# Causal attention pairs: one-pass maximum, joint weight sums, a triangle cap on VectorE and row sums of two key tiles on TensorE

## The chip, the cores and the metric

One Trainium2 chip, one of its cores. The metric is the time of one execution of the whole program in microseconds (us) on the device; the median of several runs counts.

## The reference

The program computes eight residual layers over `x` of 4 x 1024 x 128. The change touches the fifth, the latent causal attention, with 16 heads for each of 4 sequences of 1024 tokens:

```python
q = (x @ Wq + bq).reshape(Bv, Tv, N_HEAD, HEAD_DIM)
k = (x @ Wk + bk).reshape(Bv, Tv, N_HEAD, LATENT)
v = (x @ Wv + bv).reshape(Bv, Tv, N_HEAD, LATENT)
qc = jnp.einsum('bthd,dl->bthl', q, Wc)
att = jnp.einsum('bthl,bshl->bhts', qc, k) * SCALE
att = jnp.where(causal[None, None], att, -jnp.inf)
att = jax.nn.softmax(att, axis=-1)
y = jnp.einsum('bhts,bshl->bthl', att, v).reshape(Bv, Tv, N_HEAD * LATENT)
return y @ Wo + bo
```

The folded query and key have 8 numbers a head, the value 64. Softmax needs, for each of the 1024 queries, the largest score among the keys up to the query itself, the exponentials of the scores less this maximum, their sum, and their product with the values.

## The kernel before

The heads are worked off in 32 pairs. The function is `attend_pairs`; it writes out the program of each engine by hand (`tensor`, `vector`, `scalar`, `gpsimd`, `sync`), and each runs 35 steps n = 0 to 34. In step n the engines work on three pairs at once: pair n (first scores and maxima), pair n-2 (second scores, exponentials, products with the values, sums) and pair n-3 (its last products and its row sums). The instructions wait for each other through counting semaphores; each engine takes its own strictly in order.

For a pair, each of the two heads (h = 0, 1):

- **First scores**, L1594, called f0 to f15 here (8 query tiles of 128 for each head, in the order 3, 5, 1, 7, 2, 6, 0, 4): TensorE makes the scores of one query tile against all keys up to its end, 128 to 1024 columns of bf16. f(m) waits for maximum m-2, since two places in PSUM take turns.
- **Maximum**, VectorE: L1775 adds the triangle mask to the 128 columns on the diagonal in PSUM; after a wait L1777 reduces the whole row to its negated maximum. The mask add reads PSUM and one operand in SBUF.
- GpSimd splits the maxima into bf16 parts (L1797, L1799), TensorE turns them (L1638), and a DMA lays them into the query stack, so that the second scores come out with the maximum subtracted.
- **Second scores**, L1604, called s0 to s23: transposed, key tile by query half. There are 12 units u for a head pair, (key tile, query half) = (0,0), (0,1), (1,0), (1,1), (2,0), (2,1), (3,0), (3,1), (4,1), (5,1), (6,1), (7,1), with 512, 512, 384, 512, 256, 512, 128, 512, 512, 384, 256, 128 columns; s(2u+h) belongs to unit u. Units 0, 2, 4, 6, 8, 9, 10, 11 cross the diagonal; for each of their two matmuls L1608 adds a mask of 128 columns by a second matmul.
- **Exponential**, L1734, ScalarE: PSUM to fp32 weights in SBUF; units 0 and 1 go straight into the accumulator `acc`, the others into a ring `prob` of 5 units.
- **Products with the values**, L1620, called w0 to w5 (units 2c and 2c+1, both heads, fp32): w(c) waits until both units' exponentials are there.
- **Sums of weights**, L1526: GpSimd adds units 2 to 11 into `acc`, one head at a time, 20 instructions a pair. In the last pair VectorE does the second head, after everything else. A ring place is free when its unit has been added and multiplied.
- **Row sums**, L1630: TensorE multiplies `acc` by ones into four strips of 32 rows. ScalarE copies them out (L1751), as it does the products (L1717).

TensorE's order in a full step: f0, s0 to s2, f1, s3, w5 (pair n-3), s4, f2, s5, s6, f3, s7, f4, w0, f5, s8, s9, f6, row sums (pair n-3), s10, s11, f7, w1, s12, f8, s13, s14, f9, the turned shift, w2, f10, s15, f11, s16, s17, f12, s18, w3, s19, s20, f13, s21, f14, w4, f15, s22, s23.

`early.invert` (L2087, L2057, L2059) forms the reciprocals of the sums of the first three sequences on VectorE. `project_qkv` stands in front of the pairs in the same block and makes queries, keys and values; `wide_attention_output` follows.

Of the kernel before, what the change touches and what calls it, by code (L numbers as in the profile page):

```python
# [101 lines left out]
def make_constants(nc, S, pool, made):  # L102
# [21 lines left out]
    for m, sign in ((S.mask_qk, -1), (S.mask_kq, 1)):  # L124
        c.run(nc.gpsimd.memset(m[:], 0.0))
        c.run(nc.gpsimd.affine_select(out=m[:], in_=m[:], compare_op=ALU.is_ge, fill=MASKED, base=0,
                                      pattern=[[sign, P]], channel_multiplier=-sign))
# [410 lines left out]

def by_tile(v):

    return v.rearrange("p (t e) -> p t e", e=E)
# [354 lines left out]
def project_qkv(nc, S, space, wq, bq, scale, wk, bk, wv, bv, vd, ahead, v_room=None):  # L896
# [8 lines left out]
    xn = sb("xn", [P, 2, GROUP])  # L905
# [541 lines left out]
def attend_pairs(nc, S, space, early):  # L1447
# [11 lines left out]
    ADDS = 2 * (NU - FIRST)  # L1459
# [23 lines left out]
    (s1_mm, maxed, split, m_mm, m_read, s2_mm, exped, pv_mm, added, last_added, also_added, sum_mm, sum_read, o_read0, o_read1) = [  # L1483
        steps(n) for n in ("s1_mm maxed split m_mm m_read s2_mm exped pv_mm added last_added also_added sum_mm sum_read o_read0 "
# [5 lines left out]
    cleared, chain, qk_masked = sem("cleared"), sem("chain"), sem("qk_masked")  # L1490
# [11 lines left out]

    def bank(what, c):

        return S2 + (len(turns) * c + turns.index(what)) % RING2
# [5 lines left out]
    def wait_for_added(eng, j, n, h):  # L1511

        if j.c < NP - 1:
            added.wait(eng, j.times(ADDS, 2 * n + h))
# [3 lines left out]
    def add(eng, op_of, j, u, h):  # L1518
        kt, c = units[u]
        exped.wait(eng, j.times(2 * NU, 2 * u + h))  # L1520
        if kt == 1:
            pv_mm.wait(eng, j.times(2 * NU, 2 * c + h))
        else:
            wait_for_added(eng, j, units.index((kt - 1, c)) - FIRST, h)
        sums = acc[:, j.slot(2), h, c, offset(u):GROUP]
        op_of.tensor_tensor(sums, sums, weights(j, u, h), ALU.add).then_inc(added_for(j, h).sem, 1)  # L1526
# [37 lines left out]
    def attach(project):  # L1564
# [17 lines left out]
        def tensor(pe):  # L1582
# [15 lines left out]
            def second_scores(j, t):  # L1598
# [3 lines left out]
                diagonal = kt * P >= c * GROUP  # L1602
                wait_for_bank(pe, t, j.c)
                op = nc.tensor.matmul(ps[:, bank(t, j.c), o:GROUP], ks[j.slot(4)][:, h, kt * P:(kt + 1) * P],  # L1604
                                      qs[j.slot(4)][:, h, c * GROUP + o:(c + 1) * GROUP], start=True,
                                      stop=not diagonal)
                if diagonal:
                    op = nc.tensor.matmul(ps[:, bank(t, j.c), o:o + P], S.ident_b[:], S.mask_kq[:],  # L1608
# [1790 lines left out]
```

## Time and profile before

| | us |
|---|---|
| median of 3 runs | 3065.84 |
| lowest, highest run | 3062.51, 3071.13 |
| span of the profiled execution | 3008.7 |
| this layer's pairs in it | 1294 to 1962 |

What lies between the span (first to last instruction) and the run's time is outside the instructions. The profile's engines are PE (TensorE matmul), PEld (TensorE weight load), DVE (VectorE), ACT (ScalarE), POOL (GpSimd) and SPq (the queue that issues DMAs). Matmuls are pipelined, so their recorded times overlap; how long one holds TensorE is read from start to start. An operation's line is the line in the code above.

### The profile page before, as it was taken

Reading aid. Unit: us, or ns where it says so; the run is one execution under the profiler, and the core shown is the slowest. Engines: PE = TensorE matmul, PEld = TensorE weight load, DVE = VectorE, ACT = ScalarE, POOL = GpSimd, SP = SyncE. Lnnn points to the kernel's source line nnn. Section 1 sums busy time; section 2 is a strip of 40 time slices with the busy share of each in tenths; the row PEclk is TensorE's granted clock in tenths of the full one; section 3 lists DMA queues with packets and bytes.
Section 4 is the critical chain, followed back from the end, with each engine's and each line's share of the span. In section 5 each row is a group of like instructions: output and inputs, shape, how many; then the busy total and the mean of one; then the engine's idle time right before and its main releaser. Section 6 shows DMA issues by size and latency. Waiting matters only on the chain. (4 is left out here: it accounts for less than half of the span.)

```text
span 3008.7 us, 44190 instructions
## 1 busy us (share of the span) xinstructions
PE 2506.9 (83%) x13254; PEld 1086.0 (36%) x13254; DVE 2417.9 (80%) x4200; ACT 1891.9 (63%) x3760; POOL 1257.2 (42%) x1704
## 2 busy tenths in 40 slices
PE   6897799999999899969999999996846566666666
PEld 4544122222222354424444444375821111111366
DVE  7777888888888467878888888776459999999963
ACT  2213688888888521226666666604649999999864
POOL 2015433433334101529999999911732121200036
PEclk9999899999999899979999999996979999999879
DMA  4002322222233200642222222254221111111123
GB/s 101 1 1 88 93 75 74 74 74 74 75 106 108 58 1 1 209 158 81 82 87 87 88 89 89 81 210 137 78 80 42 44 41 43 42 43 32 36 73 90
DMA packets 193930, 229.15 MB, mean 76 GB/s; under 512 B 55824, under 2 KB 122128, under 8 KB 193248
## 3 DMA queue, kind: packets, MB, share of 16 engines
q1 hardware_dynamic: 158960, 193.15, 20.0%
q0 software_dynamic: 31360, 30.05, 3.9%
q10 hardware_dynamic: 3376, 3.15, 0.4%
q8 instruction: 109, 1.79, 0.2%
q14 instruction: 125, 1.02, 0.1%
HBM read 139.72 MB, written 87.95 MB: 76 GB/s over the span
## 5 line engine op out<-in xcount | busy, mean ns | idle before, releaser
L1349 DVE TENSOR_REDUCE neg_max<-ps 128x1 f32<-128x1024 f32 x512 | 602.0, 1219 | 98.7 <-PE ps L1242 90.4
L1322 ACT ACTIVATE prob<-ps 128x512 f32<-128x512 f32 x1024 | 556.3, 601 | 94.3 <-PE ps L1256 85.6
L2650 DVE TENSOR_REDUCE neg_max<-ps 128x1 f32<-128x1024 f32 x512 | 581.0, 1211 | 13.8 <-PE ps L2444 13.7
L1526 POOL TENSOR_TENSOR acc<-acc,prob 128x384 f32<-128x384 f32 (+1 forms) x630 | 572.3, 952 | 34.3 <-PE ps L1620 33.2
L2520 ACT ACTIVATE ps<-ps,neg_max 128x1024 f32<-128x1024 f32 x512 | 557.4, 1091 | 23.9 <-DVE neg_max L2650 23.0
L2444 PE MATMUL ps<-k_stack,q_stack 128*128 128x512 bf16 x1024 | 332.9, 413 | 236.7 <-ACT ps L2520 216.0
L1734 ACT ACTIVATE prob<-ps 128x512 f32<-128x512 f32 (+3 forms) x640 | 270.6, 474 | 216.0 <-PE ps L1608 159.1
L1777 DVE TENSOR_REDUCE neg_max<-ps 128x1 f32<-128x512 f32 (+7 forms) x512 | 388.0, 758 | 17.5
L1256 PE MATMUL ps<-q_stack,k_stack 128*128 128x512 bf16 x1024 | 312.2, 386 | 7.1 <-DMA k_low<-k_parts 4.9
L1266 PE MATMUL ps<-prob,v 128*32 128x512 f32 x2048 | 281.3, 621 | 0.9 <-ACT prob L1322 0.7
L2444 PEld LDWEIGHTS ps<-k_stack,q_stack 128*128 128x128 bf16 x1024 | 62.6, 99 | 501.8 <-ACT ps L2520 423.2
L1594 PE MATMUL ps<-k_stack,q_stack 72*128 72x512 bf16 (+3 forms) x768 | 216.3, 339 | 27.5 <-DVE neg_max L1777 17.4
L1775 DVE TENSOR_TENSOR ps<-ps,mask_qk 128x128 f32<-128x128 f32 x512 | 150.8, 294 | 98.5 <-PE ps L1594 95.1
L668 PE MATMUL ps<-f_wd,hT 128*128 128x512 f32 x512 | 227.3, 595 | 2.3 <-DVE other L807 2.3
L1620 PE MATMUL ps<-prob,v 128*64 128x512 f32 (+3 forms) x1280 | 228.0, 477 | 0.9 <-ACT prob L1734 0.9
L1604 PE MATMUL ps<-q_stack,k_stack 128*128 128x512 bf16 (+3 forms) x768 | 220.0, 330 | 0.9 <-ACT prob L1734 0.3
L1256 PEld LDWEIGHTS ps<-q_stack,k_stack 128*128 128x128 bf16 x1024 | 78.6, 97 | 322.1 <-ACT prob L1322 211.4
L1364 POOL TENSOR_TENSOR shift<-neg_max,zeros 128x8 bf16<-128x8 f32 x64 | 12.5, 195 | 417.8 <-DVE neg_max L1349 417.8
L1241 PE MATMUL ps<-k_stack,q_stack 64*128 64x512 bf16 x512 | 163.3, 391 | 18.9 <-DVE neg_max L1349 11.6
L1242 PE MATMUL ps<-k_low,q_low 64*128 64x512 bf16 x512 | 163.3, 391 | 0.0
L851 POOL TENSOR_TENSOR x_res<-x_res,other 128x128 f32<-128x128 f32 x64 | 29.7, 464 | 261.6 <-DVE other L807 261.6
L668 PEld LDWEIGHTS ps<-f_wd,hT 128*128 128x128 f32 x512 | 94.9, 190 | 115.3 <-issue 108.1
(365 smaller groups left out, 3932.7 us busy)
## 6 DMA issues: line engine op xcount, KB each, us to landing
q_stack<-q_parts SPq DMA_DIRECT2D x576, 48.0 KB
k_stack<-k_parts SPq DMA_DIRECT2D x576, 48.0 KB
o_quads<-o_out SPq DMA_DIRECT2D x64, 256.0 KB
v<-v_wide SPq DMA_DIRECT2D x32, 512.0 KB
o_pairs<-o_out SPq DMA_DIRECT2D x64, 256.0 KB
num<-o_pairs SPq DMA_DIRECT2D x8, 2048.0 KB, 8.5
q_parts<-parts SPq DMA_DIRECT2D x24, 384.0 KB, 2.5
k_parts<-parts SPq DMA_DIRECT2D x24, 384.0 KB, 2.7
```

The source lines that it names most:

```text
L668: op = nc.tensor.matmul(ps[:, YB + 2 * (k % 2) + half, :], hT[:, g % 2, f, k * P:(k + 1) * P], S.f0_wd[:, f, half * GROUP:(half + 1) * GROUP],
L1256: nc.tensor.matmul(ps[:, bank(n), :], ks[j.slot(4)][:, kt * P:(kt + 1) * P], qs[j.slot(4)][:, c * GROUP:(c + 1) * GROUP], start=True, stop ...
L1266: nc.tensor.matmul(ps[quad:quad + VW, OB, :], vs[j.slot(4)][:, :, kt], prob[:, n % RING, :], start=kt < 2, stop=kt >= KTS - 2).then_inc(pv ...
L1322: nc.scalar.activation(prob[:, m % RING, :], ps[:, bank(m), :], ACT.Exp).then_inc(exped.sem, 1)
L1349: nc.vector.tensor_reduce(neg_max[:, i.slot(2), m:m + 1], ps[:, first:first + 2, :].rearrange("p b n -> p (b n)"), AX.X, ALU.max, negate=T ...
L1526: op_of.tensor_tensor(sums, sums, weights(j, u, h), ALU.add).then_inc(added_for(j, h).sem, 1)
L1620: nc.tensor.matmul(ps[h * VD:(h + 1) * VD, OB + c, offset(u):GROUP], v, weights(j, u, h), start=kt == 0, stop=kt == (c + 1) * GROUP // P - ...
L1734: nc.scalar.activation(weights(j, u, h), ps[:, bank(t, j.c), offset(u):GROUP], ACT.Exp).then_inc(exped.sem, 1)
L1777: nc.vector.tensor_reduce(neg_max[:, i.slot(2), m // KTS, qt:qt + 1], ps[:, bank:bank + c + 1, :].rearrange("p b n -> p (b n)") [:, 0:(qt ...
L2444: op = nc.tensor.matmul(ps[:, bank, :], qs[n % 4][:, qt * P:(qt + 1) * P], ks[n % 4][:, c * GROUP:(c + 1) * GROUP], start=True, stop=True)
L2520: nc.scalar.activation(s, s, ACT.Exp, bias=neg_max[:, n % 2, qt:qt + 1], accum_out=sums[:, cols(n * KTS + qt, 1)]).then_inc(summed.sem, 1)
L2650: nc.vector.tensor_reduce(neg_max[:, n % 2, qt:qt + 1], ps[:, first:first + 2, :], AX.XY, ALU.max, negate=True).then_inc(maxed.sem, 1)
```

## The change

- The mask add and the reduction of a query tile become one VectorE instruction over the whole row: it adds a strip (zeros, and the triangle in its last 128 columns), negates, writes the row back to PSUM and leaves the minimum of it, which is the negated maximum.
- The mask matmuls L1608 go. Instead VectorE takes the minimum of the exponentials and a triangle (`cap_kq`: huge where the key is allowed, 0 elsewhere) in the 128 diagonal columns of both heads, in place, in SBUF. This is a "cap"; there are 8 in a pair, placed between the maxima by `caps_after` (cap 11 in front of maximum 1 of the next step). Products and sums of these units wait for the cap instead of the exponential.
- GpSimd adds units 2 to 9 alone, both heads in one instruction: 8 instead of 20 a pair. In the last pair it adds the first head, and VectorE the second, spread over the step.
- TensorE makes the row sums of units 10 and 11 from the weights themselves, by four more matmuls onto the row sums.
- ScalarE's exponentials of units 5 and 6 wait for the previous pair's row sums where they waited for its adds of units 10 and 11.
- `early.invert` moves to step 32, after maximum 10's place.
- The projection's `xn` takes the memory of `o_out`.

```diff
@@ make_constants
-    for m, sign in ((S.mask_qk, -1), (S.mask_kq, 1)):
-        c.run(nc.gpsimd.memset(m[:], 0.0))
-        c.run(nc.gpsimd.affine_select(out=m[:], in_=m[:], compare_op=ALU.is_ge, fill=MASKED, base=0,
+    c.run(nc.gpsimd.memset(S.mask_strip[:], 0.0))
+    c.run(nc.gpsimd.memset(S.cap_kq[:], -MASKED))
+    for m, sign, fill in ((S.mask_strip[:, SEQ - P:SEQ], -1, MASKED), (S.cap_kq[:], 1, 0.0)):
+        c.run(nc.gpsimd.affine_select(out=m, in_=m, compare_op=ALU.is_ge, fill=fill, base=0,
                                       pattern=[[sign, P]], channel_multiplier=-sign))
+def bcast_heads(v):
+    return v.rearrange("p (o n) -> p o n", o=1).broadcast_to([P, 2, v.shape[1]])
@@ attend_pairs
-    ADDS = 2 * (NU - FIRST)
+    LAST = NU - 2
+    ADDS = LAST - FIRST
...
+    BOTH = slice(0, 2)
+    diagonals = [u for u, (kt, c) in enumerate(units) if kt * P >= c * GROUP]
+    CAPS = len(diagonals)
+    caps_after = {1: (0,), 4: (2,), 6: (4,), 9: (6,), 12: (8, 9), 15: (10,)}
+    adds_after = {6: (2, 4), 9: (4, 6), 12: (6, 8), 15: (8, 10)}
+
+    def wait_for_weights(eng, j, u, h):
+        if u in diagonals:
+            capped.wait(eng, j.times(CAPS, diagonals.index(u)))
+        else:
+            exped.wait(eng, j.times(2 * NU, 2 * u + h))
...
-    def add(eng, op_of, j, u, h):
+    def add(eng, op_of, j, u, heads):
         kt, c = units[u]
-        exped.wait(eng, j.times(2 * NU, 2 * u + h))
+        last = 1 if heads == BOTH else heads
+        wait_for_weights(eng, j, u, last)
...
-        sums = acc[:, j.slot(2), h, c, offset(u):GROUP]
-        op_of.tensor_tensor(sums, sums, weights(j, u, h), ALU.add).then_inc(added_for(j, h).sem, 1)
+        sums = acc[:, j.slot(2), heads, c, offset(u):GROUP]
+        op_of.tensor_tensor(sums, sums, weights(j, u, heads), ALU.add).then_inc(added_for(j, last).sem, 1)
@@ second_scores
-                if diagonal:
-                    op = nc.tensor.matmul(ps[:, bank(t, j.c), o:o + P], S.ident_b[:], S.mask_kq[:],
-                                          start=False, stop=True)
@@ weigh
-                exped.wait(pe, j.times(2 * NU, 4 * couple + 3))
                 for u in (2 * couple, 2 * couple + 1):
+                    wait_for_weights(pe, j, u, 1)
@@ sum_up
+                wait_for_weights(pe, j, NU - 1, 1)
...
+                for u in range(LAST, NU):
+                    for h in (0, 1):
+                        t = h * CH + units[u][1]
+                        op = nc.tensor.matmul(ps[t * 32:(t + 1) * 32, bank("sums", j.c + 1), offset(u):GROUP], ones[:],
+                                              weights(j, u, h), start=False, stop=u == NU - 1)
@@ vector
+            def cap(j, u):
+                exped.wait(dve, j.times(2 * NU, 2 * u + 1))
+                triangles = weights(j, u, BOTH)[:, :, 0:P]
+                nc.vector.tensor_tensor(triangles, triangles, bcast_heads(S.cap_kq[:]), ALU.min
+                                        ).then_inc(capped.sem, 1)
+
             def step(i, n):
                 for m in range(NQ):
+                    if m == 1 and there(n, 3):
+                        cap(i - 3, NU - 1)
                     if there(n, 0):
...
-                        c, at = divmod(qt * P, GROUP)
-                        own = ps[:, bank + c, at:at + P]
-                        nc.vector.tensor_tensor(own, own, S.mask_qk[:], ALU.add).then_inc(qk_masked, 1)
-                        dve.wait_ge(qk_masked, i.times(NQ, m + 1))
-                        nc.vector.tensor_reduce(neg_max[:, i.slot(2), m // KTS, qt:qt + 1],
...
+                        nc.vector.tensor_tensor_reduce(row, row, S.mask_strip[:, SEQ - width:SEQ], scale=-1.0,
+                                                       scalar=-MASKED, op0=ALU.add, op1=ALU.min,
+                                                       accum_out=neg_max[:, i.slot(2), m // KTS, qt:qt + 1]
+                                                       ).then_inc(maxed.sem, 1)
+                    if m in caps_after and there(n, 2):
+                        for u in caps_after[m]:
+                            cap(i - 2, u)
+                        if n - 2 == NP - 1 and m >= 6:
+                            for u in range(*adds_after[m]):
+                                add(dve, nc.vector, i - 2, u, 1)
+                    if m == 10 and n == NP:
+                        early.invert(dve)
             run(dve, step)
-            early.invert(dve)
-            for u in range(FIRST, NU):
-                add(dve, nc.vector, Head(0, NP - 1), u, 1)
@@ gpsimd
-                    for u in range(FIRST, NU):
-                        for h in (0, 1):
-                            if h == 0 or n - 2 < NP - 1:
-                                add(pool, nc.gpsimd, i - 2, u, h)
+                    for u in range(FIRST, LAST):
+                        add(pool, nc.gpsimd, i - 2, u, BOTH if n - 2 < NP - 1 else 0)
```

## Rows read from the trace of the kernel before

**Rows 1.** Busy time by stretch: window, length, engines (instructions), TensorE clock, DMA, GB/s.
```profile
1340.00:1920.00 580.00, 578.11 (x3581) 237.76 (x3581) 477.96 (x950) 353.28 (x830) 545.55 (x649) 1.00 0.26 84
```

**Rows 2.** Lines L1594 and L1604 alone: min/median/max ns, first and last start.
```profile
L1594 PE MATMUL ps<-k_stack,q_stack x768: 217/377/634, 1294.2 to 1923.6; 72*128 72x512 bf16 x128, 72*128 72x384 bf16 x64
...
L1604 PE MATMUL ps<-q_stack,k_stack x768: 217/377/631, 1337.7 to 1958.7; 128*128 128x512 bf16 x64, 128*128 128x256 bf16 x64, 128*128 128x384 bf16 x32, 128*128 128x128 bf16 x32
```

**Rows 3.** Timeline of PE, 1500 to 1517 us: start, us, instructions merged by line.
```profile
1500.95 0.55 PE L1594 MATMUL ps<-k_stack,q_stack 72*128 72x512 bf16 x2
...
1512.09 1.72 PE L1620 MATMUL ps<-prob,v 128*64 128x512 f32 x8
...
1514.09 0.22 PE L1608 MATMUL ps<-mask_kq,ident_b 128*128 128x128 bf16 x1
1514.14 0.22 PE L1604 MATMUL ps<-q_stack,k_stack 128*128 128x128 bf16 x1
...
1516.09 0.87 PE L1620 MATMUL ps<-prob,v 128*64 128x256 f32 x8
1516.89 0.34 PE L1604 MATMUL ps<-q_stack,k_stack 128*128 128x384 bf16 x1
```

**Rows 4.** Timeline of the weight loads in front of f1.
```profile
1515.44 0.11 PEld L1594 LDWEIGHTS ps<-k_stack,q_stack 72*128 72x128 bf16 x2 [0.38 <-DVE neg_max L1777]
```

**Rows 5.** Timeline of POOL, 1500 to 1521 us.
```profile
1500.30 18.07 POOL L1526 TENSOR_TENSOR acc<-acc,prob 128x384 f32<-128x384 f32 x20 [0.96 <-PE ps L1620]
...
1519.80 1.96 POOL L1526 TENSOR_TENSOR acc<-acc,prob 128x384 f32<-128x384 f32 x2 [0.96 <-PE ps L1620]
```

**Rows 6.** Timeline of DVE, 1501 to 1517 us.
```profile
1501.54 0.30 DVE L1775 TENSOR_TENSOR ps<-ps,mask_qk 128x128 f32<-128x128 f32 x1 [0.38 <-PE ps L1594]
...
1515.31 0.29 DVE L1775 TENSOR_TENSOR ps<-ps,mask_qk 128x128 f32<-128x128 f32 x1
1515.63 0.69 DVE L1777 TENSOR_REDUCE neg_max<-ps 128x1 f32<-128x512 f32 x1
1516.24 0.29 DVE L1775 TENSOR_TENSOR ps<-ps,mask_qk 128x128 f32<-128x128 f32 x1
```

**Rows 7.** Lines L1775 and L446 alone: min/median/max ns, first and last start.
```profile
L1775 DVE TENSOR_TENSOR ps<-ps,mask_qk x512: 289/294/300, 1294.7 to 1923.9; 128x128 f32<-128x128 f32 x171
...
L446 DVE SCALAR_TENSOR_TENSOR kv<-kv,kneg x8: 679/688/1432, 20.0 to 84.8; 128x512 f32<-128x512 f32 x8
```

**Rows 8.** Groups by form, POOL, 1500 to 1600 us: busy us, mean ns.
```profile
L1526 POOL TENSOR_TENSOR acc<-acc,prob 128x512 f32<-128x512 f32 x41 | 51.1, 1274 | 0.0
...
L1526 POOL TENSOR_TENSOR acc<-acc,prob 128x128 f32<-128x128 f32 x20 | 8.7, 456 | 0.0
```

**Rows 9.** Timelines of DVE, single instructions with two SBUF operands, 1928 to 1961 us.
```profile
1928.79 1.40 DVE L2059 TENSOR_TENSOR sums<-sums,thirds 96x512 f32<-96x512 f32 x1
...
1945.54 6.96 DVE L1526 TENSOR_TENSOR acc<-acc,prob 128x384 f32<-128x384 f32 x1 [11.11 <-PE ps L1620]
...
1953.29 1.49 DVE L1526 TENSOR_TENSOR acc<-acc,prob 128x256 f32<-128x256 f32 x1
...
1960.37 0.29 DVE L1526 TENSOR_TENSOR acc<-acc,prob 128x128 f32<-128x128 f32 x1
```

**Rows 10.** Timelines of POOL beside them, 1946 to 1952 us and at 1953.4 us.
```profile
1945.75 6.34 POOL L1526 TENSOR_TENSOR acc<-acc,prob 128x256 f32<-128x256 f32 x8
...
1952.78 1.72 POOL L1526 TENSOR_TENSOR acc<-acc,prob 128x512 f32<-128x512 f32 x1
```

**Rows 11.** Timelines of PE and DVE at the stage's start and end.
```profile
1319.20 1.25 PE L1594 MATMUL ps<-k_stack,q_stack 72*128 72x512 bf16 x3 [7.47 <-DMA v<-v_wide]
...
1924.93 3.34 DVE L2087 RECIPROCAL sums<-sums 96x512 f32<-96x512 f32 x1
...
1933.05 1.38 DVE L2057 CAST thirds<-sums 96x512 bf16<-96x512 f32 x1
```

## What the change is expected to do to the time

> **What bounds the kernel now.** I read the page's engine totals first, then the busy times by stretch, and last the timelines of single rounds, because the shares of the whole span mix six layers. The change touches one stage, 1294 to 1962 us. In its steady part, 1340 to 1920 us, TensorE (PE) is busy 578.11 of 580 us at a granted clock of 1.00, GpSimd (POOL) 545.55, VectorE (DVE) 477.96 and ScalarE (ACT) 353.28 [rows 1]. Pair rounds run from 1337.7 us (first second-score matmul) to 1923.6 us (last first-score matmul), 30 rounds, so 19.53 us each [rows 2].
>
> Is that PE share real? A matmul's recorded length overlaps the next one's, so the reader should look at starts. A mask matmul starts at 1514.09 and the next matmul 0.05 us later [rows 3], the pace of 128 columns at 2.4 GHz; the only gap of note that I find in a round is about 0.2 us in front of f1, where PE waits for the maximum of tile 15 [rows 4]. So PE sets the round. POOL is just behind: its 20 adds take 18.07 us without a pause, and then it waits 0.96 us for PE's next products [rows 5]. DVE has about 3.4 us of slack in a round, all of it waiting for scores.
>
> **PE's part.** Removed: 16 mask matmuls of 0.055 us from start to start [rows 3], 0.88 us a round. Added: row sums of units 10 and 11, 256 and 128 columns, two heads, fp32. The nearest row is w5, which moves exactly these columns: it starts at 1516.09 and the next matmul at 1516.89, 0.80 us, of which about 0.1 is the change of weights and tile shape that the sums pay already [rows 3]. So 0.64 to 0.80, taken 0.70. PE's own need falls from 19.33 (without the 0.2 us wait) to 19.15 us.
>
> **DVE's part.** A query tile now costs 0.32 us for the mask (1515.31 to 1515.63), then its columns at 0.96 per ns and 0.08 us (512 columns: 0.61 from 1515.63 to 1516.24) [rows 6]. The fused instruction streams the same columns once and no trace row shows it. Bounds: no dearer than the reduction alone, or a second small instruction of 0.29 us more [rows 7]. I take the first, since the reduction too ends by writing one column, and get 0.21 us for 128 columns, 0.61 for 512, 1.15 for 1024: 5.1 us less a round, at worst 0.5 less. The Trainium skill ("VectorE: DVE Perf Modes", section "Two Vector instructions with no wait between them") says that an op which also writes its accumulator is two instructions, the main one and a read of the accumulator; no run here shows it, and by it the sum would lie towards the upper of my two ends.
> Added are 8 caps of 2x128 columns, 256/0.96 + 80 = 0.35 us each, 2.8 us a round. So DVE's own work falls by some 2 us. But each cap waits for ACT's exponential, the next tile's maximum is queued behind it, and f(m+2) waits for that; and w0 to w5 and POOL's adds now wait for caps.
>
> **POOL's part.** Adds of 128 and 512 columns take 456 and 1274 ns [rows 8]: 2.13 ns a column and 0.18 us fixed, less 0.05 us of overlap when queued (20 adds in 18.07 us [rows 5]). A joint add of two heads then takes 0.68 us (unit 6), 1.22 (4), 1.77 (2, 9) and 2.31 (3, 5, 7, 8); together 14.7 us where 18.1 stood. This saves nothing by itself, since POOL was waiting for PE.
>
> **What decides: caps and adds exclude each other.** A cap reads two operands from SBUF, which no DVE instruction of a steady round does today; the mask adds read one and stay at 289 to 300 ns beside a busy POOL [rows 7]. The trace has two-operand DVE instructions beside these very POOL adds in two places. At the stage's end DVE adds 256 columns in 1.49 us, where 128 columns without POOL take 0.29, so 256 about 0.43 [rows 9]; it ends 0.28 us after the POOL add that began at 1952.78, and that POOL add was itself stretched from 1.27 to 1.72 us [rows 8, 10]. And DVE's subtraction of bf16 from fp32 in 1928.79, a cap's operand types, takes 1.40 us [rows 9] where 512 columns with two SBUF operands take 0.68 at best [rows 7]. So a cap waits for the POOL add under way, and a POOL add for the cap; the joint adds make the thing waited for up to 2.3 us long.
>
> I walk one round, from the end of cap 9 as 0, with about 0.05 us for a hand-over.
> - POOL adds 8 and 9: 0.1 to 4.2. Meanwhile PE does w4 (1.7, [rows 3]) and f15, whose scores arrive 0.5 us later (f5 at 1500.95 reached DVE at 1501.54 [rows 3, 6]); the maximum of tile 15 ends near 3.0. Cap 10 then waits for add 9 and ends at 4.5.
> - Maximum 0 (0.61) and cap 11 (0.35) end at 5.5. Only now may w5 run (0.80); f2 comes after it and s4, and its scores arrive at 6.9. f3 arrives at 7.7 behind s5 and s6; maxima 3 (1.15) and 4 (0.48), cap 2 (0.35): 9.8 with the hand-over.
> - Adds 2 and 3 (4.1), cap 4 (0.3), adds 4 and 5 (3.5), cap 6 with its hand-over (0.4), adds 6 and 7 (3.0), caps 8 and 9 (0.65): 21.75. Cap 6 is ready near 16.8 and cap 8 near 20.0, each while the odd add of the pair in front still runs, so these waits are real.
>
> PE is not what closes this loop: its waits are some 2.6 us a round, about 1.9 of them at w5 and the rest at f12 and w4. The round grows from 19.53 to 21.75: 2.2 us, times 30 rounds 67 us.
> Ends of that price. Low: a cap holds POOL up by only 0.2 us (the 512-column one at 1952.78 cost 0.45) and the stretch from cap 10 to cap 2 is 0.3 shorter: 21.0, 44 us. High: the fused maximum costs 0.29 more, which lengthens that stretch by up to 1.0, and add 8 starts ahead of cap 9, as eight queued adds passed a waiting DVE add of 6.96 us [rows 9, 10], which moves w4 and f15 back, 1.1 more: 63 us beyond 67.
> The Trainium skill ("SBUF — State Buffer", section "SBUF: two separate sides") speaks against this change: a DVE op with two SBUF inputs and a GpSimd op that reads SBUF share one port pair, and whichever starts first holds it for its whole length. By that rule alone a cap waits for one add, the sum of 21.75. The trace agrees for the 1.49 us add, but for the 6.96 us DVE add it does not; by that row the high end is the nearer one.
>
> **Ends of the stage.** The first pair's maxima lie in front of a 7.47 us wait for the second pair's load, so they gain nothing; the second pair's saves up to 5 us, taken 3 [rows 11]. At the end the reciprocals, 9.5 us of DVE from 1924.93 to 1934.43 [rows 11], ran when DVE had nothing else; now they stand between cap 6 and cap 8 of the pair before the last, where POOL covers 3 us, so about 6.5 us late. Against it POOL has less to add in the last two rounds, and the last sums need no adds of units 10 and 11. Together -4 to +12, taken +4. No DMA changes; the projection's buffer shared with the output's is free by then, and the longer mask is one POOL memset at the kernel's start: nothing, and at most 1 us without cover.
>
> **Sum.** The profiled execution spans 3008.7 us, 57.1 less than the median of 3065.84, which lies outside the span and stays. 3008.7 + 67 - 3 + 4 = 3075.7, and with the 57.1 it is 3133 us. With both ends of the price and of the stage's ends this case's own range is 3100 to 3205.
>
> **Rivals.**
> - Caps slip between the adds. If a cap does not wait for POOL (bf16 and a repeated operand might read otherwise), one stall stays: f15 to its scores 0.5, maximum 15 0.75, cap 10 0.35, maximum 0 0.61, cap 11 0.45 make 2.7 us up to w5, while PE needs 1.9 to get there. A round is 19.15 + 0.8 = 19.95: 12 us more over 30 rounds; with 3 off at the start and 2 at the end, 3073. For it: no row shows a cap. Against it: the 1.40 us row.
> - Faster. PE is the bound and loses 0.88 us for 0.70, and the 0.2 us wait goes, because the fused maximum of tile 15 ends earlier. This gives 0.2 to 0.4 us a round, 9 us, and 3 and 4 at the ends: 3050. It decides only if caps 10 and 11 are done before PE reaches w5, 1.9 us after f15, and no cap waits for POOL by more than the 3 us of slack that DVE has. For it: PE's share [rows 1]. Against it: the 2.7 us chain alone is too long.
> - The change relieves POOL, as it says, but that is no gain: 14.7 us of adds and 8 caps of 0.3 that shut POOL out are 17.1 of the 18.1 us before. This is within the forecast.
>
> **How the numbers follow.** The forecast has 0.64, the first rival 0.18, the faster one 0.18. A measurement here can tell about 0.3%, 9 us: faster is below 3057, slower above 3075. The first rival lies at that upper edge, two thirds of it inside. So faster 0.18, same 0.12, slower 0.70. Range 3058 to 3205: it takes in the forecast with its ends and the first rival, and leaves out the faster one.
>
> **What would show it.** Right: caps of 0.4 us alone but 1 to 2.5 us in the mean on DVE; POOL busy under 80%; PE waiting for DVE at w5, w4 and f12, some 2.5 us a round; rounds of 21 to 23 us. Wrong: caps near 0.43 us throughout and rounds under 20 us would refute the exclusion; a fused maximum of over 1.5 us at 1024 columns would mean that DVE bounds and my walk is too short.

## The result, and the profile after

| | before | after |
|---|---|---|
| median | 3064.42 us (4 runs) | 3124.57 us (4 runs, 3118.84 to 3126.04) |
| ratio | | 1.0188, interval [1.0172, 1.0204] |
| pairs' stage, first to last matmul | 1294.2 to 1961.8, 667.6 us | 1296.9 to 2024.6, 727.7 us |
| of it, one round | 19.53 us | 21.37 us |

The change costs 60 us, and in the two profiled executions the stage alone is 60.1 us longer, so the price lies in this stage. The first view is the busy time of the steady stretch; its line answers [rows 1] (window, length, PE, PEld, DVE, ACT, POOL, clock, DMA, GB/s).

```profile
1340.00:1920.00 580.00, 535.30 (x3042) 195.99 (x3041) 538.67 (x1084) 322.62 (x758) 421.45 (x270) 1.00 0.24 77
```

TensorE was busy throughout and is not any more. GpSimd is busy 124 us less (18.4 us a round before, 15.5 after). VectorE, whose program has one instruction a tile instead of two, shows 61 us more: the time that a held instruction waits counts as busy here, as the caps below show. No engine is full and the clock is unchanged at 1.00, so the engines wait for one another. The rounds come from the lines of the two score matmuls, as in [rows 2]:

```profile
L1624 PE MATMUL ps<-q_stack,k_stack x768: 217/377/634, 1338.1 to 2019.8; 128*128 128x512 bf16 x64, 128*128 128x256 bf16 x64, 128*128 128x384 bf16 x32, 128*128 128x128 bf16 x32
L1615 PE MATMUL ps<-k_stack,q_stack x768: 217/377/634, 1296.9 to 1979.1; 72*128 72x512 bf16 x128, 72*128 72x384 bf16 x64
```

From 1338.1 (first second score) to 1979.1 (last first score) are 30 rounds, 21.37 us each. Of the 60.1 us, 55 are the rounds, 2.3 us are won at the start (43.5 to 41.2 us before the first second score) and 7.3 lost at the end (38.2 to 45.5 us after the last first score).

Now the caps (line L1795) alone: min/median/max in ns.

```profile
L1795 DVE TENSOR_TENSOR prob<-prob,cap_kq x224: 410/1439/2620, 1343.8 to 2022.0; 128x256 f32<-128x256 f32 x112
L1795 DVE TENSOR_TENSOR acc<-acc,cap_kq x32: 411/414/430, 1341.1 to 2005.0; 128x256 f32<-128x256 f32 x32
```

Same form, same size: cap 0 (on `acc`) always takes 0.41 us, the others up to 2.62. One round of POOL and the caps in it, from their timelines (start, us, idle time before it and what ended that):

```profile
1505.78 4.42 POOL L1547 TENSOR_TENSOR acc<-acc,prob 128x1024 f32<-128x1024 f32 x2 [0.36 <-DVE prob L1795]
...
1515.31 4.13 POOL L1547 TENSOR_TENSOR acc<-acc,prob 128x768 f32<-128x768 f32 x2 [4.46 <-DVE prob L1795]
1519.81 3.58 POOL L1547 TENSOR_TENSOR acc<-acc,prob 128x512 f32<-128x512 f32 x2 [0.36 <-DVE prob L1795]
1523.75 3.04 POOL L1547 TENSOR_TENSOR acc<-acc,prob 128x256 f32<-128x256 f32 x2 [0.36 <-DVE prob L1795]
1527.15 2.47 POOL L1547 TENSOR_TENSOR acc<-acc,prob 128x1024 f32<-128x1024 f32 x1 [0.36 <-DVE prob L1795]
```

```profile
1508.64 1.84 DVE L1795 TENSOR_TENSOR prob<-prob,cap_kq 128x256 f32<-128x256 f32 x1
...
1511.01 0.41 DVE L1795 TENSOR_TENSOR prob<-prob,cap_kq 128x256 f32<-128x256 f32 x1
...
1512.22 0.41 DVE L1795 TENSOR_TENSOR acc<-acc,cap_kq 128x256 f32<-128x256 f32 x1
...
1514.81 0.42 DVE L1795 TENSOR_TENSOR prob<-prob,cap_kq 128x256 f32<-128x256 f32 x1
...
1517.15 2.58 DVE L1795 TENSOR_TENSOR prob<-prob,cap_kq 128x256 f32<-128x256 f32 x1
...
1522.18 1.48 DVE L1795 TENSOR_TENSOR prob<-prob,cap_kq 128x256 f32<-128x256 f32 x1
...
1525.63 1.78 DVE L1795 TENSOR_TENSOR prob<-prob,cap_kq 128x256 f32<-128x256 f32 x2
```

Adds 8 and 9 run to 1510.20; cap 10, ready at 1508.64, ends at 1510.48. Caps 11, 0 and 2 fall into POOL's pause and take 0.41. Adds 2 and 3 end at 1519.44 and cap 4, which could start at 1517.15, as add 3 did, at 1519.73. In the whole stage 126 of the 256 caps were held, and each of them ended 0.28 or 0.29 us after the add that it met. After caps 4, 6 and 8 POOL waits, 0.36 us from the end of one add to the start of the next, because the next add needs that cap's result. But for the two short splits of the maxima POOL adds nothing from 1510.20 to cap 2's end: a pause of 5.11 us to the next add at 1515.31. And TensorE (the gap in brackets is what it waited):

```profile
1505.75 1.72 PE L1636 MATMUL ps<-prob,v 128*64 128x512 f32 x8 [0.34 <-DVE prob L1795]
...
1510.53 0.65 PE L1636 MATMUL ps<-prob,v 128*64 128x256 f32 x4 [0.98 <-DVE prob L1795]
1511.48 0.44 PE L1636 MATMUL ps<-prob,v 128*64 128x128 f32 x4 [0.29 <-DVE prob L1795]
```

These are w4 and the two halves of w5, each let go by a cap.

### The profile page after: what moved, and what is told of

It is laid out like the page before. It is cut to its first block and busy times, and to the rows that moved or that the text cites. A ratio compares the mean times of both kernels' runs of the same rounds, so it can differ in the third digit from the quotient of the medians.

```text
span 3124.3 us, 43247 instructions
## 1 busy us (share of the span) xinstructions
PE 2547.2 (82%) x12998; PEld 1086.1 (35%) x12998; DVE 2520.4 (81%) x4454; ACT 1886.6 (60%) x3760; POOL 1168.2 (37%) x1330
## 5 line engine op out<-in xcount | busy, mean ns | idle before, releaser
L1547 POOL TENSOR_TENSOR acc<-acc,prob 128x1024 f32<-128x1024 f32 (+4 forms) x256 | 475.1, 1871 | 185.6 <-DVE prob L1795 168.7
L2479 PE MATMUL ps<-k_stack,q_stack 128*128 128x512 bf16 x1024 | 343.5, 424 | 226.1 <-ACT ps L2555 204.4
L1809 DVE CUSTOM_DVE_ANT_0 ps<-ps,mask_strip 128x512 f32<-128x512 f32 (+7 forms) x512 | 379.9, 773 | 63.7 <-PE ps L1615 57.0
L1636 PE MATMUL ps<-prob,v 128*64 128x512 f32 (+3 forms) x1280 | 236.4, 482 | 54.5 <-DVE prob L1795 54.4
L1795 DVE TENSOR_TENSOR prob<-prob,cap_kq 128x256 f32<-128x256 f32 x224 | 264.9, 1194 | 16.4 <-ACT prob L1759 16.4
L1624 PE MATMUL ps<-q_stack,k_stack 128*128 128x512 bf16 (+3 forms) x768 | 205.6, 331 | 1.5 <-ACT prob L1759 1.2
L1247 PE MATMUL ps<-k_stack,q_stack 64*128 64x512 bf16 x512 | 163.7, 392 | 19.1 <-DVE neg_max L1355 12.5
L3146 PE MATMUL ps<-w_f_w,hT 128*128 x624 | 99.6, 311 | 54.4 <-ACT hT L3190 52.2
L801 DVE SCALAR_TENSOR_TENSOR x_res<-ps,comb,x_res 128x128 f32<-128x128 f32 x256 | 87.8, 343 | 58.7 <-PE ps L674 58.1
```

Of the source, the lines that this page charges most:

```text
L1547: op_of.tensor_tensor(sums, sums, weights(j, u, heads), ALU.add).then_inc(added_for(j, last).sem, 1)
L1636: nc.tensor.matmul(ps[h * VD:(h + 1) * VD, OB + c, offset(u):GROUP], v, weights(j, u, h), start=kt == 0, stop=kt == (c + 1) * GROUP // P - ...
L1795: nc.vector.tensor_tensor(triangles, triangles, bcast_heads(S.cap_kq[:]), ALU.min).then_inc(capped.sem, 1)
L1809: nc.vector.tensor_tensor_reduce(row, row, S.mask_strip[:, SEQ - width:SEQ], scale=-1.0, scalar=-MASKED, op0=ALU.add, op1=ALU.min, accum_o ...
L2479: op = nc.tensor.matmul(ps[:, bank, :], qs[n % 4][:, qt * P:(qt + 1) * P], ks[n % 4][:, c * GROUP:(c + 1) * GROUP], start=True, stop=True)
```

## The experiments

Rounds are read as above, from the two lines of score matmuls; from one f0 to the next in the steady part they differ from these by at most 0.05 us. Ratios are against the kernel before measured on the same chip with that run, where its median was 3063.2 to 3067.3 us.

| kernel | median us | ratio, interval | round us | stage us |
|---|---|---|---|---|
| before | 3064.4 | | 19.53 | 667.6 |
| after | 3124.6 | 1.0188 [1.0172, 1.0204] | 21.37 | 727.7 |
| after, one-operand caps | 3062.6 | 0.9983 [0.9972, 0.9994] | 19.32 | 666.7 |
| the same, written back | 3062.6 (one run) | | 19.34 | 664.1 |
| the same, plain | 3090.8 (one run) | | 20.47 | 700.0 |
| after, mask matmuls for caps | 3074.7 | 1.0026 [1.0014, 1.0038] | 19.95 | 676.9 |
| before, fused maximum | 3058.4 | 0.9965 [0.9951, 0.9980] | 19.33 | 659.5 |
| before, row sums | 3084.0 | 1.0066 [1.0051, 1.0082] | 20.17 | 685.7 |
| before, joint adds | 3061.3 | 0.9995 [0.9986, 1.0005] | 19.53 | 666.3 |
| after, single adds | 3110.6 | 1.0142 [1.0125, 1.0159] | 20.94 | 714.3 |
| after, all caps but 10, 11 | 3077.8 | 1.0043 [1.0028, 1.0058] | 19.88 | 680.3 |
| after, caps 10, 11 alone | 3101.3 | 1.0122 [1.0093, 1.0151] | 20.87 | 706.5 |
| mask in PSUM, joint adds | 3131.6 | 1.0223 [1.0200, 1.0246] | 21.63 | 735.5 |
| caps 0, 2, fused, joint | 3054.2 | 0.9962 [0.9949, 0.9976] | 19.37 | 659.8 |

### Is it the second operand?

**The cap as a one-operand instruction**, same place, same waits, same 2 x 128 columns:

```diff
-                nc.vector.tensor_tensor(triangles, triangles, bcast_heads(S.cap_kq[:]), ALU.min
-                                        ).then_inc(capped.sem, 1)
+                nc.vector.tensor_reduce(cap_room[:, diagonals.index(u)], triangles, AX.X, ALU.max).then_inc(capped.sem, 1)
```

> The kernel after, with each cap replaced by a maximum over the same 2x128 columns that reads one operand from SBUF and writes two numbers beside it; order, waits and semaphores stay as they are. The triangle of the second scores is left out of the weights, so the output isn't the reference's. Theory (a cap and a POOL add exclude each other because the cap reads two SBUF operands): the instruction takes about 0.35 us and waits for nobody, POOL's adds run undisturbed, and only the chain f15, maximum 15, cap 10, maximum 0, cap 11, w5 is left: a round of 19.3 to 20.0 us, taken 19.7 where the kernel after has 21.37; 30 x 1.67 = 50 us less than after, 3075 us, 0.3% over the kernel before. Rival (any instruction between the maxima closes the loop, by its place in DVE's order and its waits): round stays over 21 us, 3115 to 3125 us.

Round 19.32 us, 3062.6 us, at the low end of the rounds expected and below the 3075 us: 2.05 us of a round vanish with the second operand. The line of this instruction, and POOL beside it:

```profile
L1796 DVE TENSOR_REDUCE cap_room<-prob x224: 407/416/421, 1342.2 to 1957.2; 128x2 f32<-128x256 f32 x112
```

```profile
1505.12 6.81 POOL L1548 TENSOR_TENSOR acc<-acc,prob 128x1024 f32<-128x1024 f32 x3 [0.31 <-ACT prob L1760]
...
1515.82 4.14 POOL L1548 TENSOR_TENSOR acc<-acc,prob 128x768 f32<-128x768 f32 x2 [3.41 <-DVE cap_room L1796]
```

The longest of the 224 takes 0.421 us, so none waited, and POOL's pause (1511.93 to 1515.82) is 3.89 us instead of 5.11. The rest of POOL's round, adds and yields, is 19.32 - 3.89 = 15.4 us against 21.37 - 5.11 = 16.3. So the exclusion lengthens POOL's stretch of adds by 0.8 us and its pause by 1.2, together 2.05. Without it the change would have been 0.2 us a round ahead.

**Or is it the writing?** The reduction writes two numbers, a cap writes 256 columns back. So once more, in place:

```diff
+                nc.vector.tensor_scalar(triangles, triangles, -MASKED, None, op0=ALU.min, op1=ALU.max,
+                                        accum_out=cap_room[:, diagonals.index(u):diagonals.index(u) + 1]).then_inc(capped.sem, 1)
```

> The kernel after with each cap replaced by an instruction that reads the 2x128 columns as its only SBUF tensor, takes the minimum with a constant that changes nothing, writes them back in place and leaves a maximum beside them. The triangle is left out of the weights, so the output isn't the reference's. Theory (the second SBUF operand is what excludes POOL): 0.35 to 0.45 us for each, no waiting, round 19.3 to 19.6 us, as in the one-operand run, 3063 to 3070 us. Rival (writing the 2x128 columns back into SBUF is what collides, which the one-operand run left out): mean over 1 us, round 21 us or more, 3115 us.

```profile
L1796 DVE TENSOR_SCALAR_CACHE_REDUCE prob<-prob x224: 406/415/421, 1343.6 to 1958.0; 128x256 f32<-128x256 f32 x112
L1796 DVE DVE_READ_ACCUMULATOR prob<-prob x224: 77/82/85, 1343.9 to 1958.4; 128x1 f32 x112
```

19.34 us, longest 0.421: writing back is not what collides.

**The plain form** of the same instruction, without the second result:

```diff
+                nc.vector.tensor_scalar(triangles, triangles, -MASKED, None, op0=ALU.min).then_inc(capped.sem, 1)
```

> The kernel after with each cap replaced by a minimum with a constant that changes nothing, in place, 2x128 columns, one SBUF operand, and no second result (the run before left a maximum beside it). The triangle is left out of the weights, so the output isn't the reference's. Theory (only a second tensor read from SBUF excludes POOL): no waiting, at most 0.42 us each, round 19.3 us, 3063 us. Rival (this plain form may stream faster by reading through both ways into SBUF, and so exclude POOL with one operand as well): each 0.2 to 0.3 us alone, 1 us or more in the mean, round 20.8 to 21.4 us, 3105 to 3125 us. The Trainium skill, page SBUF — State Buffer, section SBUF: two separate sides, counts an op in a two-port mode with those of two SBUF inputs, so by it the rival holds if this form runs in such a mode.

```profile
L1795 DVE TENSOR_SCALAR prob<-prob x224: 279/1087/2454, 1338.9 to 1988.9; 128x256 f32<-128x256 f32 x112
L1795 DVE TENSOR_SCALAR acc<-acc x32: 278/282/293, 1336.1 to 1972.2; 128x256 f32<-128x256 f32 x32
```

My theory falls in its narrow wording. With one SBUF operand, but at a faster pace (0.28 us where the form above takes 0.41), it is held up to 2.45 us, and the round is 20.47; each of the 126 that were held ended 0.15 us after the add that it met. The rival had the mechanism and set the round a little too high (20.8 to 21.4); that the instruction is shorter than a cap would explain it, but was not tested. So the count of operands alone does not decide. The Trainium skill ("VectorE: DVE Perf Modes", section "What auto-detection actually checks") says that, where firmware enables it for the instruction, the engine takes a double-rate mode over both ports if a single source and the destination lie in SBUF and their outer dimensions are both even or equal; with the rule of "SBUF — State Buffer", section "SBUF: two separate sides", that such an op shares the ports with GpSimd's, this run agrees.

### What each part is worth

**After with mask matmuls instead of caps** (the second scores' code of before, weights waited for through the exponential):

```diff
-            if u in diagonals:
-                capped.wait(eng, j.times(CAPS, diagonals.index(u)))
-            else:
-                exped.wait(eng, j.times(2 * NU, 2 * u + h))
+            exped.wait(eng, j.times(2 * NU, 2 * u + h))
```

> The kernel after without caps: TensorE's 16 mask matmuls are back, everything else of the change stays (fused maximum, joint adds, row sums of units 10 and 11 on TensorE, the reciprocals' new place). Theory (caps make the loss): TensorE bounds again with 19.33 us of its own work plus 0.70 for the added row sums, 20.0 us a round at most, 19.8 if part of the row sums' price is hidden: 30 x (21.37 - 19.95) = 43 us less than after, 3080 us, 3075 to 3088. Rival (the longer joint adds or the fused maximum make it): round over 20.8 us, over 3107 us.

19.95 us, the value expected; 3074.7 us, just under the range expected, since the stage's end is 8.5 us shorter as well (45.5 to 37.0). The joint adds and the fused maximum are cleared; caps for mask matmuls cost 1.42 us a round.

**The fused maximum alone** in the kernel before: L1775 and L1777 become the one instruction of the change.

> The kernel before with the fused maximum alone (and the memory of the projection's xn as in the kernel after). Theory: TensorE still bounds, so DVE's 5 us a round are worth only the 0.2 us wait in front of f1 and about 2 to 3 us at the stage's start: round 19.3 to 19.5 us, 3055 to 3062 us. Rival (DVE's maxima are on the path for more than that): round under 19.1 us, under 3050 us; or the fused instruction is dearer than the reduction it replaces where it counts: 3064 us or more.

19.33 us, 3058.4 us, 0.35% faster: the 0.2 us wait in front of f1 and 2.2 us at the start (43.5 to 41.3), as expected.

**The row sums of units 10 and 11 alone**, in the kernel before:

```diff
+                for u in range(LAST, NU):
+                    for h in (0, 1):
+                        t = h * CH + units[u][1]
+                        op = nc.tensor.matmul(ps[t * 32:(t + 1) * 32, bank("sums", j.c + 1), offset(u):GROUP], ones[:],
+                                              weights(j, u, h), start=False, stop=u == NU - 1)
```

> The kernel before with the row sums of units 10 and 11 made by TensorE alone (POOL adds units 2 to 9, one head at a time). Theory: four fp32 matmuls more on the bound engine, 0.62 to 0.70 us a round, 19.53 + 0.65 = 20.2 us, 3083 to 3087 us. Rival (the relief of POOL takes away waits of about the same size): 19.6 to 19.8 us, 3066 to 3074 us.

20.17 us, 3084.0 us: +0.64 a round on the engine that bounds, all of it visible.

**Joint adds alone**, in the kernel before:

```diff
-                        for h in (0, 1):
-                            if h == 0 or n - 2 < NP - 1:
-                                add(pool, nc.gpsimd, i - 2, u, h)
+                        add(pool, nc.gpsimd, i - 2, u, BOTH if n - 2 < NP - 1 else 0)
```

> The kernel before with joint adds alone: POOL adds both heads of all ten units in one instruction each. Theory: POOL has over a microsecond less to do in a round but was not what bounds, so the round stays at 19.4 to 19.6 us and the time at 3060 to 3070 us. Rival (longer adds let ring places come free later and ScalarE's exponentials wait): 19.7 us or more, 3070 us or more.

19.53 us, ratio 0.9995: POOL's busy time in the steady stretch fell from 545.55 [rows 1] to 510.50 us, and nothing came of it.

In a round: fused maximum -0.20, joint adds 0, row sums +0.62 to 0.64, caps for mask matmuls +1.42. That sums to 21.37, but by construction: 1.42 is the kernel after less the run with mask matmuls, and 0.62 that run less the one with the fused maximum. Measured on their own are the row sums (0.64), the joint adds and the fused maximum.

### Which caps carry the price

**Without caps 10 and 11**, whose four mask matmuls come back:

```diff
+    diagonals = [0, 2, 4, 6, 8, 9]
+    masked = [10, 11]
```

> The kernel after with TensorE's mask matmuls back for units 10 and 11 alone (4 a round) and no caps 10 and 11; the six other caps stay. Theory (the price is closed by the way from cap 9 over the maxima and caps 10 and 11 to w5, and so to cap 2 and POOL's next add): from cap 2 to cap 9 the kernel after takes 12.2 us and keeps them; from cap 9 to cap 2 it takes 9.2, and where nothing holds caps up (the one-operand run) 7.7, with 0.2 for the mask matmuls 7.9: a round of 20.0 us, 19.6 to 20.3, 3083 us. Rival (each of the eight caps carries about the same share of the 2.05 us between the one-operand run and the kernel after): 19.3 + 0.2 + 6 x 0.26 = 21.0 us a round, 3113 us.

19.88 us, inside the theory's range, a whole microsecond below the rival's. Against the one-operand run (19.32 + 4 x 0.055 = 19.54) the six caps that are left cost 0.34 us; against TensorE's own work, from the run with all mask matmuls (19.95 - 12 x 0.055 = 19.29), they cost 0.59. Read from start to start, TensorE loses 0.18 us in front of f12 and 0.31 in front of w4 against that run. The caps wait as long as before:

```profile
L1802 DVE TENSOR_TENSOR prob<-prob,cap_kq x160: 409/1441/2630, 1346.5 to 1974.2; 128x256 f32<-128x256 f32 x160
```

```profile
1497.74 4.43 POOL L1549 TENSOR_TENSOR acc<-acc,prob 128x1024 f32<-128x1024 f32 x2 [0.36 <-DVE prob L1802]
...
1505.76 4.13 POOL L1549 TENSOR_TENSOR acc<-acc,prob 128x768 f32<-128x768 f32 x2 [3.04 <-DVE prob L1802]
...
1517.61 4.43 POOL L1549 TENSOR_TENSOR acc<-acc,prob 128x1024 f32<-128x1024 f32 x2 [0.36 <-DVE prob L1802]
```

POOL's adds take 16.28 us from 1505.76 to 1522.04, as in the kernel after; its pause is 3.59 instead of 5.11 us. The round lost that 1.5. Here the waits between POOL's adds cost the round little of their length, and what lies between its last add and the next first one counts in full.

**Caps 10 and 11 alone**:

```diff
+    diagonals = [10, 11]
+    masked = [0, 2, 4, 6, 8, 9]
```

> The counterpart: caps 10 and 11 stay, the six others are mask matmuls again (12 a round). Theory: TensorE's own round is 19.95 (run with all mask matmuls) less 4 x 0.055 = 19.73; there add 9 ends 1.0 us after maximum 15, so cap 10 waits that long, maximum 0 and cap 11 follow, and what comes behind w5 is late by about 0.9: 20.6 us a round, 20.2 to 21.0, 3102 us. Rival (equal shares): 19.73 + 2 x 0.26 = 20.25, 3091 us. Second rival (without the six other caps the two no longer meet an add): 19.8, 3077 us.

20.87 us, 3101.3 us: the theory's 20.6 (20.2 to 21.0), not 20.25. Two caps cost 1.14 us over the 19.73 that TensorE needs. On the same base all eight cost 21.37 - (19.95 - 0.88) = 2.30 us, 0.6 more than the six (0.59) and the two (1.14) together: the two groups make each other dearer. TensorE's waits for w5's halves stand in its timeline:

```profile
1503.67 0.65 PE L1643 MATMUL ps<-prob,v 128*64 128x256 f32 x4 [0.55 <-DVE prob L1802]
1504.61 0.44 PE L1643 MATMUL ps<-prob,v 128*64 128x128 f32 x4 [0.29 <-DVE prob L1802]
```

**Single adds** in the kernel after, 16 for 8:

```diff
-                        add(pool, nc.gpsimd, i - 2, u, BOTH if n - 2 < NP - 1 else 0)
+                        for h in (0, 1):
+                            if h == 0 or n - 2 < NP - 1:
+                                add(pool, nc.gpsimd, i - 2, u, h)
```

> The kernel after with POOL's joint adds split into one for each head (16 instead of 8 a pair), caps unchanged. Rival (the price is the length of the instruction that a cap waits for): caps 4, 6, 8 and 10 each wait about half as long, some 0.5 to 1.2 us less each, and the round falls to 19.5 to 20.4 us, 3070 to 3095 us. Theory (what closes the loop is POOL's whole work plus the caps that it yields to and its pause at cap 2; a cap that waits shorter only lets POOL add sooner what it has to add anyway): 8 more instructions cost POOL about 8 x 0.1 = 0.8 us, and only the cap in front of w5 comes earlier, about 0.6: round 21.2 to 21.8 us, 3118 to 3138 us.

20.94 us, between the two expectations, so both sizes were wrong. POOL's timeline shows the terms:

```profile
1504.64 4.78 POOL L1547 TENSOR_TENSOR acc<-acc,prob 128x512 f32<-128x512 f32 x4
...
1513.59 16.81 POOL L1547 TENSOR_TENSOR acc<-acc,prob 128x384 f32<-128x384 f32 x16 [3.52 <-DVE prob L1795]
```

The adds take 16.81 instead of 16.28 us (+0.53, I had 0.8), the pause 1509.42 to 1513.59 is 4.17 instead of 5.11 (-0.94, I had 0.6): cap 10 now ends 0.9 us before the last add instead of 0.28 after it. Net -0.41, measured -0.43. The mean of the seven caps on `prob` falls from 1.23 to 0.76 us, 3.2 us of VectorE's time a round, and the round gains 0.43: again the waits between the adds hardly count, the one in front of w5 does. But the joint adds, free in the kernel before, do cost 0.43 in the kernel after.

This run also shows the exclusion from POOL's side, since here the next add is often one that needs no cap and is queued already. One cap, and three adds of 512 columns each, the last undisturbed:

```profile
1503.78 1.18 DVE L1795 TENSOR_TENSOR prob<-prob,cap_kq 128x256 f32<-128x256 f32 x1 [0.24 <-ACT prob L1759]
```

```profile
1503.22 1.45 POOL L1547 TENSOR_TENSOR acc<-acc,prob 128x512 f32<-128x512 f32 x1
1504.64 1.45 POOL L1547 TENSOR_TENSOR acc<-acc,prob 128x512 f32<-128x512 f32 x1
1506.06 1.26 POOL L1547 TENSOR_TENSOR acc<-acc,prob 128x512 f32<-128x512 f32 x1
```

The cap starts during the first add and ends 0.29 us after it; the second add, whose start is recorded before that, takes 1.45 us instead of 1.26. (The first is longer too, by the cap before this one.) All 155 held caps of this run end 0.28 or 0.29 us after the add under way; in 123 cases an add stood queued behind it, and that add was 0.18 or 0.19 us longer in the median. No queued add got in ahead of a waiting cap.

### Two versions meant to be faster

**The mask added in PSUM by VectorE**, one SBUF operand, before the exponential (fused maximum, joint adds, no added row sums, no mask matmuls):

```diff
+            def mask(j, t):
+                u, h = divmod(t, 2)
+                s2_mm.wait(dve, j.times(2 * NU, t))
+                own = ps[:, bank(t, j.c), offset(u):offset(u) + P]
+                nc.vector.tensor_tensor(own, own, S.cap_kq[:], ALU.add).then_inc(capped.sem, 1)
```

> A version meant to keep what the change saves TensorE and avoid the caps: fused maximum, joint adds of all ten units on POOL, no added row sums, no mask matmuls; DVE adds the mask to the 128 diagonal columns of the second scores in PSUM (one SBUF operand) ahead of the exponential, 16 times a round, between the maxima in TensorE's order. If nothing new waits, TensorE's round is 19.33 - 0.88 = 18.45 us, DVE has 11.0 + 16 x 0.29 = 15.6 us to do: round 18.5 to 18.8 us, 3035 to 3045 us. Rival (the way second score, mask, exponential, bank free is longer by a mask and by the maximum queued in front of it, and with three banks TensorE waits): over 19.5 us a round, 3065 to 3110 us. I hold the rival for as likely.

21.63 us, 3131.6 us: the rival, and beyond its range. The mask itself is cheap and never held (the longest of 512 takes 0.334 us), but TensorE now waits for free banks. The two longest lines of the waits in the steady stretch (who waits for whom: us, times, longest):

```profile
ACT prob L1760 <- DVE ps L1797: 229.3, 187, 3.2
PEld ps L1622 <- ACT prob L1760: 139.5, 187, 1.8
```

ScalarE waits for the mask, and TensorE's second scores for ScalarE.

**Caps where POOL pauses**: units 0 and 2 alone, with the fused maximum and all ten units' joint adds, no added row sums.

```diff
+    diagonals = [0, 2]
+    masked = [4, 6, 8, 9, 10, 11]
```

> A version from what the runs show: fused maximum, joint adds of all ten units on POOL, no added row sums, mask matmuls for units 4, 6, 8, 9, 10, 11, and caps for units 0 and 2 alone, which fall into POOL's pause and stand in front of no wait of TensorE's that is near. TensorE's round: 19.33 (fused maximum alone) less 4 x 0.055 = 19.1 us, POOL has about 17 us of adds: round 19.1 to 19.2, 3050 to 3055 us, 3 to 8 us below the fused maximum alone. Rival (POOL's first add now starts behind cap 2 and its last ones end later, so that caps 0 and 2 of the next pair meet them): round 19.3 to 19.8, 3058 to 3072 us.

3054.2 us, ratio 0.9962 [0.9949, 0.9976]: faster than both kernels, by as much as the fused maximum alone (0.9965). The round is 19.37, not 19.1 to 19.2: the four saved mask matmuls bring nothing. Cap 0 met adds here:

```profile
1511.18 1.09 DVE L1802 TENSOR_TENSOR acc<-acc,cap_kq 128x256 f32<-128x256 f32 x1
1514.24 0.41 DVE L1802 TENSOR_TENSOR prob<-prob,cap_kq 128x256 f32<-128x256 f32 x1
```

That is the rival's mechanism, and the starts of TensorE's matmuls tell its share. Maximum 2 stands behind cap 0 and ends at 1512.62, and f4, which waits for it, starts at 1512.73, 0.38 us after s7 instead of 0.22. These 0.16 us are most of the 0.22 saved; the other 0.05 are lost in front of f1.

## Why the prediction was right, point by point

3133 was said, 3124.6 measured. By its terms: rounds +67 said, 30 x 1.84 = +55.1 measured; start -3, measured -2.3; end +4, measured +7.3. So 68 was said for the stage and 60.1 measured, 7.9 too much, and the base was 1.4 higher (3065.84, now 3064.42). The sum as written is also 1 us short: 3008.7 + 68 is 3076.7. The signs named came out: caps of 0.41 us alone and 1.2 in the mean, POOL 73% busy, rounds of 21.4 us.

- **What bounds, and that it changes hands**: right. TensorE fell from 578.11 to 535.30 us in the same 580. Compared from start to start with the one-operand run, it waits 1.42 us more at w5, 0.42 at w4 and 0.18 at f12, the three places named; with 0.25 that the one-operand run waits too, that is 2.3 us a round where 2.6 were said.
- **Exclusion**: right, and shown by the one-operand run, for the caps as they stand. A cap waits for the add under way (it ends 0.28 us after it, the amount of [rows 9, 10]), and an add for the cap (1.26 to 1.45 us in the run with single adds). The rule of the Trainium skill ("SBUF — State Buffer", section "SBUF: two separate sides"), by which the first to start keeps the other out for its whole length, agrees with both. The 6.96 us row, from which I took the high end of the range, did not recur in any of 224 caps: the longest, 2.62 us, is the 2.34 of the add that it met and 0.28. Why that row was so long stays open.
- **The walk**: 21.75 against 21.37. Cap 10 ended at 4.45 after cap 9 (4.5 said), cap 11 at 5.39 (5.5), cap 2 at 9.2 (9.8), and from cap 2 to cap 9 it was 12.2 (11.95). The step that failed, in size, is "Only now may w5 run (0.80)": w5's unit 10 starts after cap 10, at 1510.53, while VectorE does maximum 0, so cap 11 holds up only the second half, and TensorE is through 0.43 us after cap 11 (1511.42 to 1511.85) instead of 0.80. That is most of the 0.6 us by which cap 2 came early; from cap 2 to cap 9 I was 0.2 short, so part of the closeness of 21.75 is luck.
- **Rival one, caps slipping between the adds**: the mechanism that it supposed was made in the one-operand run, and its price was mis-sized by the same step: 0.8 us of waiting at w5 said, 0.13 found, and 0.12 in front of f1; 19.95 us said, 19.32 measured, so 3062.6 us instead of 3073.
- **The other rivals**: the faster one's price, 0.2 us a round, is what the one-operand run shows; its condition, that no cap waits long, was not met. That POOL's relief is no gain in itself is what joint adds alone show (0).
- **TensorE's terms**: row sums 0.70 taken, 0.64 alone (0.75 from start to start in the kernel after, 1516.95 to 1517.70). The masks' removal, 0.88 by starts [rows 3], gives 19.95 - 19.32 = 0.63 where nothing excludes. The other 0.25 goes into two short waits for VectorE that the one-operand run has and the run with mask matmuls has not: f1 follows s2 after 0.33 us instead of 0.22, and w5 takes 0.94 us instead of 0.81, from its start to the next matmul's. First w5 with mask matmuls, then with one-operand caps:

```profile
1519.54 0.87 PE L1638 MATMUL ps<-prob,v 128*64 128x256 f32 x8
1520.35 0.34 PE L1622 MATMUL ps<-q_stack,k_stack 128*128 128x384 bf16 x1
```

```profile
1511.42 1.00 PE L1637 MATMUL ps<-prob,v 128*64 128x256 f32 x8
1512.36 0.34 PE L1625 MATMUL ps<-q_stack,k_stack 128*128 128x384 bf16 x1
```

  So TensorE's own need was 19.32 - 0.25 = 19.07 us, where 19.15 was said.
- **Fused maximum**: the accumulator is read by an instruction of its own, as the Trainium skill ("VectorE: DVE Perf Modes", section "Two Vector instructions with no wait between them") says; by that rule the sum would lie towards the upper end. But the next instruction starts at the same time as the read:

```profile
1510.40 0.69 DVE L1809 CUSTOM_DVE_ANT_0 ps<-ps,mask_strip 128x512 f32<-128x512 f32 x1
1511.01 0.13 DVE L1809 DVE_READ_ACCUMULATOR2_ANT neg_max<- 128x1 f32 x1
1511.01 0.41 DVE L1795 TENSOR_TENSOR prob<-prob,cap_kq 128x256 f32<-128x256 f32 x1
```

  0.61 us from start to start for 512 columns, the lower end, though there are two instructions.
- **End of the stage**: +7.3, within -4 to +12. The reciprocals stand in front of cap 8, and TensorE's w4 behind it:

```profile
1993.32 3.34 DVE L2122 RECIPROCAL sums<-sums 96x512 f32<-96x512 f32 x1
```

```profile
1999.99 3.25 PE L1636 MATMUL ps<-prob,v 128*64 128x512 f32 x8 [4.55 <-DVE prob L1795]
```

  It is the order, not the exclusion: with the two forms of one-operand caps that nothing holds the end is 45.5 and 42.6 us, and without caps, the reciprocals in the same place, it is 37.0.
- **"57.1 us outside the span"**: wrong, and so is the sentence under the table of the kernel before that puts the whole difference outside the instructions. The kernel after spans 3124.3 of 3126.04 us. Before's profiled execution was short in two later stages that the change does not touch: `expert_tiles` ran 97 us twice at a granted clock of 0.96, in after 124 and 122 us at 0.84 and 0.86. Adding the change to the median was right, the reason given was not; stage lengths should have been compared from the start.

## What to carry to other kernels

In these runs a VectorE minimum that read two SBUF tensors, or one at the faster pace (0.28 us for 0.41), took turns with GpSimd's adds. Before moving work to VectorE beside a busy GpSimd, look for such a row in the trace and try a form that is not held; here one operand in PSUM, or one at the slower pace, was not. What such a wait costs depends on its place: six caps that waited up to 2.6 us between the adds cost 0.3 to 0.6 us a round, two in front of the matmuls that the next round's first cap depends on cost 1.1, and all eight together more than that sum. And relief for an engine with slack (joint adds) is worth nothing by itself and may cost later, when something begins to wait for the longer instruction.

## What the runs showed of the hardware

The same in-place minimum over 2 x 128 fp32 columns was held up to 2.45 us by GpSimd in its plain form (0.28 us alone) and never in the form that also leaves an accumulated value (0.41 us, longest 0.421 of 224). That the form with the second result is not held I had not expected.
